# Two strided reductions and a reciprocal change places in VectorE's step list

## The reference

```python
xn = _layernorm(x, axis=-1)
x = x + attention(xn, ...) + mixture(xn, ...)
# attention: two causal softmaxes (16 heads each, 64 wide), o = a1 @ v1 - lam * (a2 @ v2), then o @ Wo
# mixture:
logits = (xn @ phi_w.T + phi_b).reshape(t, z, 64, 32)     # 64 experts, 32 slots
D = softmax(logits, axis=3)                               # dispatch: over the slots of an expert
C = softmax(logits, axis=2)                               # combine: over the experts of a slot
X = einsum('tznp,tzd->npd', D, x)                         # then clip, layernorm, tanh, expert matmul -> Y_tilde
Y = einsum('tznp,npH->tzH', C, Y_tilde)
```

## Time and profile before

| what | value |
|---|---|
| median of three runs | 1361.44 us |
| the profiled execution: its own time, and its span | 1368.9 us, 1367.1 us |
| granted TensorE clock, mean over the span | 0.981 |
| busy: TensorE, VectorE, ScalarE, GpSimd | 94%, 85%, 79%, 80% |
| longest waits of VectorE and of TensorE on one another | 89.8 us (L836 on the scores), 24.1 us (L78 on L871) |

### The profile page before, as it was taken

One profiled execution on the slowest core, in us unless ns is written; L12 is line 12 of the kernel. 1 busy time (PEld: TensorE's weight loads), 2 busy tenths in 40 slices (PEclk: granted clock), 3 DMA queues, 4 the chain that ended last, 5 costly groups with the idle time before them and its releaser, 6 DMA issues. The chain is left out here.

```text
span 1367.1 us, 29569 instructions
## 1 busy us (share of the span) xinstructions
PE 1285.3 (94%) x9136; PEld 984.6 (72%) x9136; DVE 1166.4 (85%) x3632; ACT 1084.0 (79%) x3221; POOL 1095.1 (80%) x848
## 2 busy tenths in 40 slices
PE   2899999999999999999999999999999999479998
PEld 2677777777777777777777777777777777368887
DVE  7688999889988998899889988998899888768776
ACT  4688888898888888888888888888888888355554
POOL 1468888888888788888888888888888888749994
PEclk9899999999999999999999999999999999679999
DMA  5111121112111211112111211121111117347773
GB/s 172 47 55 68 62 80 70 69 69 80 70 68 62 64 70 69 69 69 73 69 69 69 80 70 68 69 80 70 63 52 67 66 67 209 93 163 246 262 254 125
DMA packets 105980, 126.31 MB, mean 92 GB/s; under 512 B 20192, under 2 KB 56032, under 8 KB 105696
## 3 DMA queue, kind: packets, MB, share of 16 engines
q1 hardware_dynamic: 102160, 122.97, 26.5%
q10 hardware_dynamic: 3664, 1.44, 0.4%
HBM read 48.89 MB, written 35.65 MB: 62 GB/s over the span
## 5 line engine op out<-in xcount | busy, mean ns | idle before, releaser
L736 ACT ACTIVATE e<-e,neg_max 128x256 f32<-128x256 f32 (+1 forms) x1024 | 451.5, 442 | 54.0 <-DVE neg_max L836 54.0
L836 DVE CUSTOM_DVE_ANT_0 e<-ps_s,mask 128x256 f32<-128x256 f32 (+1 forms) x1024 | 294.7, 353 | 90.9 <-PE ps_s L564 89.8
L1041 POOL TENSOR_TENSOR disp<-logit,gmax 128x512 f32<-128x512 f32 x128 | 134.5, 1051 | 221.6 <-DVE gmax L878 221.5
L722 ACT ACTIVATE pT<-ps_t 128x512 f32<-128x512 f32 x384 | 226.7, 591 | 80.1 <-PE ps_t L547 79.6
L1049 POOL TENSOR_TENSOR e<-e,inv 128x1024 f32<-128x1024 f32 x128 | 284.5, 2223 | 0.0
L547 PEld LDWEIGHTS ps_t<-ident,e 128*128 128x128 f32 x1536 | 186.5, 141 | 87.2 <-issue 65.5
L547 PE MATMUL ps_t<-ident,e 128*128 128x128 f32 x1536 | 230.3, 273 | 2.6 <-ACT pT L722 1.7
L564 PEld LDWEIGHTS ps_s<-qk 64*128 64x128 f32 x2048 | 172.9, 186 | 50.1 <-issue 46.1
L564 PE MATMUL ps_s<-qk 64*128 64x256 f32 (+1 forms) x2048 | 202.4, 337 | 0.0
L736 ACT ACTIVATION_READ_ACCUMULATOR e<-e,neg_max 128x1 f32 x1024 | 191.6, 187 | 0.0
L1077 POOL TENSOR_TENSOR logit<-logit,m_all 128x512 f32<-128x512 f32 x128 | 164.8, 1288 | 0.0
(11 more groups left out here) (148 smaller groups left out, 2998.8 us busy)
## 6 DMA issues: line engine op xcount, KB each, us to landing
xs<-xT SPq DMA_DIRECT2D x128, 256.0 KB, 2.4
c_scratch<-logit SPq DMA_DIRECT2D x128, 256.0 KB, 2.0
xT<-c_scratch SPq DMA_DIRECT2D x16, 1024.0 KB, 5.5
c_back<-c_scratch SPq DMA_DIRECT2D x16, 1024.0 KB, 5.8
fx<-xT SPq DMA_DIRECT2D x64, 64.0 KB, 1.9
fxn<-xn SPq DMA_DIRECT2D x32, 64.0 KB, 1.9
xT<-in_L_ffn_expert_w SPq DMA_DIRECT2D x4, 512.0 KB, 6.2
xn<-in_L_ffn_expert_w SPq DMA_DIRECT2D x4, 512.0 KB, 7.4
```

The lines of the kernel that those rows point to most:

```text
L722: nc.scalar.activation(pT[:, k, :], ps_t[:, (q + k) % 2, :], ACT.Copy).then_inc(t_out, 1)
L736: ins = nc.scalar.activation(dst, dst, ACT.Exp, bias=neg_max[:, q, c:c + 1], scale=-1.0, accum_out=total[:, q, c:c + 1])
L836: nc.vector.tensor_tensor_reduce(out=dst, in0=part, in1=here, scale=-1.0, scalar=HIGHEST, op0=ALU.add, op1=ALU.min, accum_out=neg_max[:, q ...
L1041: nc.gpsimd.tensor_tensor(by_expert(bank_of(disp, t, jj)), by_expert(bank_of(logit, t, jj)), gmax[:, jj, :].unsqueeze(2).to_broadcast([P, ...
```

## The change

`slot_max_end` and `slot_inverse` move from step 0, between `bank_max` and `take_logits`, to step 1, between `dispatch_inverse` and `bank_max`. `slot_sum` stays in step 3 and moves from behind `bank_max` to in front of it, right behind `slot_max` and ahead of `output_low` and `values_low`. No instruction is added or removed, no wait, buffer or shape changes, and the other engines' lists are the same.

```diff
@@ -940,6 +940,11 @@
                     next_queries(it, j, 1)
                     dispatch_inverse(*back(it, j, 2))
                     slot_max(*back(it, j, 1))
+                    if j == 1:
+                        slot_max_end(it - 1)
+                        slot_inverse(it - 3)
+                    elif it < ITER + 1:
+                        slot_sum(it - 2)
                     if live(g + 1, NG) and (kk, j) == (PER - 1, 3):
                         values_low(nc, dve, env, g + 1)
                     if live(g, NG) and (kk, j) == (0, 3) and g > 0:
@@ -959,13 +964,6 @@
                     bank_max(v, j)
                 if live(g + 1, NG) and (kk, j) == (PER - 1, 2):
                     projections_low(nc, dve, env, g + 1)
-                if j == 0:
-                    slot_max_end(it - 1)
-                if j == 3:
-                    if it < ITER + 1:
-                        slot_sum(it - 2)
-                if j == 0:
-                    slot_inverse(it - 3)
                 if live(it, NTT):
                     take_logits(it, j)
                 take_slots(it - 1, j)
```

## The result

The changed kernel takes 1340.65 us (median of four runs, 1340.21 to 1345.53) against 1361.47 us: 0.9854 of the time before, 95% interval 0.9838 to 0.9869. It is 20.8 us faster. The forecast was 25 us. The granted clock is not what made it faster: from 70 to 1100 us of the span it is 1.00 in both profiles.

What follows compares the result with a forecast made beforehand. TensorE's list, with its waits for VectorE to read the logits, was taken as the bound. Gains 12.3 + 0.5 + 3.2 + 9.2 = 25.2 us, from 1361.4 to 1336 us; likeliest case 1331 to 1342, 8 in 10 1330 to 1352.

Steps and rivals of the forecast that it cites:

- What bounds the kernel: Main phase: TensorE's list sets the pace; its 24.1 us of waits in 48 places for VectorE's logits lengthen the iteration.
- Maximum and inverse: Moved into step 1's 1.96 us of VectorE idle time: 0.44 in each of 28 iterations, 12.3, plus 0.5 us.
- the rival of no change: Another loop sets TensorE's pace, so gains at `turn(0)` are waited for a little later: 1361 us; chance 0.05.
- Sum in a plain step 3: With `kk` = 1, 2 the 0.99 us sum fits in 1.30 idle: 14 x 0.23 = 3.2 us gained.
- Sum with a low half: Step 3 with `kk` = 0, 3: sum hidden in the low half's wait for GpSimd; 14 x 0.66 = 9.2 us gained.
- The limit: Step 0 behind low halves: third transposes wait for ScalarE's unmoved copy, plus 0.15 to start; gain 0.66 per place.
- The reductions beside GpSimd: Moved reductions run beside GpSimd's long multiplication; no slowdown taken, since one maximum there took 1.02 us.
- the slower rival: Strided reductions take the port pair too, over 1.3 us beside L1049: 7.4 us slower, 1369, up to 1378; chance 0.07.
- The case that only part comes back: Lock does not hide the sum in 14 low-half steps; maxima 0.99 later: 11.4 us gained, 1350; chance 0.14.
- the third rival's sum: Total for strided reductions taking the port pair as well: 7.4 us slower, 1369 us; chance 0.07.
- the first one's: Total if the lock does not hide the sum: 11.4 us gained, 1350 us; chance 0.14.
- The end: Iteration 31's gain is taken by VectorE's 2.30 us DMA wait; draining steps zero, within 1 us either way.

Runs made afterwards that it cites:

- the halves alone: Against the kernel before, only the sum moved: 1351.49 us, ratio 0.9903; only the maximum and inverse moved: 1352.01 us, ratio 0.9905.
- The run with the copy first: Changed kernel with step 1's second query copy (L842) ahead of the dispatch sum (L900): 1338.49 us, ratio 0.9817 to the kernel before.
- the runs with the other orders: Changed kernel with step 3's sum behind the low half: 1355.15 us; changed kernel with the low halves between maxima and logits: 1335.13 us.

## Why the prediction was right, and where it was off

The mechanism held at each place. The size did not quite: 25.2 us were forecast, and the stretch gave 21.4. Two terms were put too large.

*What bounds the kernel.* Right. TensorE's list set the pace, and each wait at `turn(0)` was iteration time: the halves alone shorten their own steps, and their gains add.

*Maximum and inverse: 12.8 us forecast, 10.1 measured.* This is the larger of the two misses. The distance behind `turn(0)` did fall by 0.45, but step 1 only by 0.36. TensorE's weight loads show the rest, here in steps 1 and 3 of the kernel before, and in step 1 of the changed kernel:

```profile
646.25 0.19 PEld L78 LDWEIGHTS ps_tu<-xs,a_w 128*128 128x128 f32 x1 [0.18 <-DVE qk L842]
...
663.33 0.19 PEld L78 LDWEIGHTS ps_tu<-xs,a_w 128*128 128x128 f32 x1 [0.27 <-DVE qk L842]
```
```profile
598.13 0.19 PEld L78 LDWEIGHTS ps_tu<-xs,a_w 128*128 128x128 f32 x1 [0.27 <-DVE qk L842]
```

Arriving 0.45 sooner, the fourth projection now waits for VectorE's second query copy out of the bank that it needs. Before, these weights began to load at 646.25, for a product that started at 646.35, so their short wait cost nothing; now the product starts with its weight load (598.14 and 598.13), and its second part follows after 0.33 us in place of 0.24. That is the missing 0.09. In step 3, where nothing had held TensorE up earlier, the same wait was there before the change. I wrote that TensorE shows no wait in the first half of step 3, where I had ScalarE's copies and GpSimd's products in mind; it did wait there, for VectorE, and the length of step 3, 8.91, is what step 1 has fallen to. Reading it would have given the 0.36. So the rival of no change had a small part of the truth: some of what TensorE gained at `turn(0)` it waits for a little later. The run with the copy first confirms it: step 1 at 8.80.

*Sum in a plain step 3: 3.2 us forecast, 14 x 0.22 = 3.1 measured.*

*Sum with a low half: 9.2 us forecast, 7 x 0.57 + 7 x 0.56 = 7.9 measured.* That the lock would hide the sum was right (L152 at 1.01, the maxima as late as before), and the runs with the other orders show that it is the reason. The limit was named rightly too. ScalarE's copy of `turn(0)` behind `kk` = 3 in the changed kernel, which answers to the earlier trace rows:

```profile
588.05 0.58 ACT L722 ACTIVATE pT<-ps_t 128x512 f32<-128x512 f32 x1
```

It ends at 588.63, and the third transposes start at 588.68. The weight loads of the second and of the third group in this step:

```profile
587.24 0.47 PEld L547 LDWEIGHTS ps_t<-ident,e 128*128 128x128 f32 x4
...
588.68 0.42 PEld L547 LDWEIGHTS ps_t<-ident,e 128*128 128x128 f32 x4 [0.23 <-ACT pT L722]
```

The second group's weight loads start 0.11 ahead of its first product (587.35), and it takes 0.35 to the next product; the third group's start only with it, and it takes 0.57. I had put 0.15 for the release; it is 0.05, and another 0.22 until TensorE is back in step. Behind `kk` = 0 I took the copy to stand about as near. There it ends at 622.93, the third group's weight loads start at 622.98, and the group takes 0.50: 0.14 is lost, which is what step 0 there is longer than a plain one.

*The reductions beside GpSimd: no cost.* Right: L893 took 0.99 and L915 1.05 beside the long multiplication, so the slower rival's condition, over 1.3 us, was never met; no L915 or L893 of the changed kernel takes over 1.07. The case that only part comes back has to be made by hand: it is the run with the sum behind the low half. (The prediction says that a count without the lock gives the third rival's sum. It gives the first one's, 1350: the maxima come 0.99 later in the 14 low-half steps.)

*The end.* I left iteration 31 out, since its DMA wait would take its gain. Up to its step 3 that iteration is 0.6 us shorter. In the row that answers to the earlier trace rows the wait is about as long as before:

```profile
1129.66 0.69 DVE L871 TENSOR_TENSOR logit<-ps_tu,bias 128x512 f32<-128x512 f32 x1 [2.27 <-DMA c_scratch<-logit]
```

But one row does not settle it: in the second profiled execution of the changed kernel the same wait is 1.60. Whether iteration 31 keeps its gain stays open.

## What to carry to other kernels

Put work of a helper engine into its longest wait for the engine that sets the pace, not into the gap between that wait and the result the pacing engine needs next. Before counting a recovered wait in full, look for the next wait in a step where the first one is already absent: that step's length is the floor. Where an instruction is far longer than at its shortest, find whose end it waits for: work put in front of it is free up to that end, while moving an instruction by half a microsecond, past another engine's start, can make it wait for that engine's whole instruction.

## What the runs showed of the hardware that was not expected

- The lock between VectorE and GpSimd turned a shift of half a microsecond into 1.2 us of every step 0: L887 took 0.75 us when it started 0.16 ahead of GpSimd's 1024-number multiplication, and 2.06 when it started 0.38 behind that start. The Trainium skill (SBUF — State Buffer, "SBUF: two separate sides") says that whichever starts first holds the port pair for its whole instruction; the trace agrees in both directions, with the multiplication at 2.34 when it came second and 1.89 when it came first.
- A wait of TensorE cost more than the wait itself: the transposes released 0.05 us after ScalarE's copy took 0.22 us longer to the next product (0.57 against 0.35) than a group whose weights had been loaded ahead.
